# Expert layer: three of the eight in_b heads summed by TensorE through diagonal matrices, five left on VectorE

## The reference

```
sim = einsum('pbnhd,hkpd->pbnhk', q, keys)          # q = x @ Wq.T, 2 x 8 heads, 128 keys each
indices = best pair of keys of each head            # TOPK = 1: one expert of 8192 per head
A_in, B_in, A_out, B_out = in_a[indices], in_b[indices], out_a[indices], out_b[indices]
hidden = x @ W_in.T                                 # 1024 wide
lin = einsum('bnd,bnhkd->bnhk', x, A_in) * relu(scores)
hidden = hidden + einsum('bnhk,bnhkd->bnd', lin, B_in)
hidden = gelu(hidden)
out = hidden @ W_out.T
lout = einsum('bnd,bnhkd->bnhk', hidden, A_out) * relu(scores)
out = out + einsum('bnhk,bnhkd->bnd', lout, B_out)
```

## Time and profile before

| | |
|---|---|
| runs | 2763.74 us (2760.53 to 2766.83) |
| the profiled execution | 2771.96 us |
| its span in the trace | 2770.0 us |
| VectorE busy in the span | 2087.9 us (75%) |
| TensorE busy in the span | 2423.2 us (87%) |
| TensorE's granted clock, mean | 0.972 |
| rounds of experts | 32, from about 1590 us to the end |

### The profile page before, as it was taken

The page is one execution under the profiler, slowest core; times in us unless marked ns, Lnnn a source line. Parts: engine busy times, 40 slices in busy tenths (PEclk is TensorE's granted clock), DMA queues, the critical chain, the costliest instruction groups (busy, mean ns, idle before and its releaser), DMA issues. The chain is left out here.

```text
span 2770.0 us, 47172 instructions
## 1 busy us (share of the span) xinstructions
PE 2423.2 (87%) x12792; PEld 1326.1 (48%) x12792; DVE 2087.9 (75%) x5831; ACT 1093.2 (39%) x2559; POOL 1026.1 (37%) x1486
## 2 busy tenths in 40 slices
PE   7889988989889898899885999998989898989975
PEld 4455555655556555565543644443434343434432
DVE  1567676676766667667642299999989998999998
ACT  2266666666666566666663211111111111111110
POOL 1133333233332333323231245554545444545553
PEclk9999999999999999999987999999999999999997
DMA  3044454434544445444444899998989998999996
GB/s 103 17 119 116 118 161 132 138 111 118 161 132 137 112 118 159 132 138 114 147 137 143 302 372 377 370 372 337 373 331 375 351 372 331 375 366 346 375 369 255
DMA packets 303980, 631.15 MB, mean 228 GB/s; under 512 B 162800, under 2 KB 167920, under 8 KB 303728
## 3 DMA queue, kind: packets, MB, share of 16 engines
q0 software_dynamic: 79616, 423.66, 39.8%
q1 hardware_dynamic: 190320, 103.92, 13.3%
q10 hardware_dynamic: 33792, 100.67, 11.0%
HBM read 581.99 MB, written 146.80 MB: 263 GB/s over the span
## 5 line engine op out<-in xcount | busy, mean ns | idle before, releaser
L1078 DVE CUSTOM_DVE_ANT_0 scores<-s_bank,added 128x512 f32<-128x512 f32 x512 | 350.6, 688 | 273.2 <-PE s_bank L581 190.2
L1407 PE MATMUL l_bank<-fold,xn_tf 128*128 128x512 f32 x1024 | 449.9, 592 | 2.8 <-ACT xn_tf L1482 2.8
L886 ACT ACTIVATE probs<-scores,nmx 128x512 f32<-128x512 f32 x512 | 372.8, 728 | 151.8 <-DVE nmx L1078 147.9
L1367 POOL DMA_INDIRECT out_rows<-rows_out,rows_now x256 | 270.0, 1054 | 361.2 <-DVE out_sum L1631 286.6
L892 ACT COPY prob_t<-t_bank 128x512 f32<-128x512 f32 x512 | 298.4, 583 | 211.0 <-PE t_bank L591 211.0
L519 POOL TENSOR_TENSOR added<-mask_add,band 128x136 f32<-128x136 f32 (+1 forms) x512 | 245.9, 482 | 363.5 <-DVE nmx L1078 362.2
L1358 POOL DMA_INDIRECT in_rows<-rows_in,rows_now x256 | 296.1, 1157 | 224.9 <-PE hid_ps L1429 135.6
L591 PE MATMUL t_bank<-ident,probs 128*128 128x128 f32 x2048 | 316.4, 282 | 8.8 <-ACT cv L864 4.1
L591 PEld LDWEIGHTS t_bank<-ident,probs 128*128 128x128 f32 x2048 | 235.4, 142 | 180.9 <-issue 104.5
L1611 DVE CUSTOM_DVE_ANT_0 out_rows<-out_rows,hid,gates 128x1024 f32<-128x1024 f32 x256 | 320.0, 1279 | 2.7 <-ACT hid L1509 2.7
L1495 ACT COPY sims<-l_bank 128x512 f32<-128x512 f32 x128 | 74.2, 580 | 626.4 <-PE l_bank L1407 626.4
(11 more groups left out here) (177 smaller groups left out, 3607.4 us busy)
## 6 DMA issues: line engine op xcount, KB each, us to landing
rows_in<-in_in_b_dram ACTq DMA_DIRECT2D x16, 2048.0 KB, 9.2
rows_out<-in_out_a_dram ACTq DMA_DIRECT2D x16, 2048.0 KB, 9.2
rows_in<-in_in_a_dram ACTq DMA_DIRECT2D x16, 1024.0 KB, 5.7
rows_out<-in_out_b_dram ACTq DMA_DIRECT2D x16, 1024.0 KB, 5.5
x_scratch<-x SPq DMA_DIRECT2D x32, 512.0 KB, 7.4
rel_scratch<-rel_pad SPq DMA_DIRECT2D x16, 640.0 KB, 3.3
band<-rel_scratch SPq DMA_DIRECT2D x512, 20.0 KB, 2.1
prob_scratch<-probs SPq DMA_DIRECT2D x512, 20.0 KB, 2.4
```

Of the source, the lines that this page charges most:

```text
L886: nc.scalar.activation(prob_tile(s % PSLOTS), scores[:, s % 2, :], ACT.Exp, bias=nmx[:, s:s + 1], scale=-1.0, accum_out=lsum[:, s:s + 1]). ...
L1078: nc.vector.tensor_tensor_reduce(out=scores[:, s % 2, :], in0=s_bank[s % HPT][:, 0:L], in1=added[:, s % 2, :], scale=-1.0, scalar=-NEG, op ...
L1367: nc.gpsimd.indirect_dma_start(out_rows[:, h, :], None, rows_out, bass.IndirectOffsetOnAxis(rows_now[:, odd, h:h + 1], 0)).then_inc(out_lo ...
L1407: ins = nc.tensor.matmul(l_bank[c % 2][:], xn_t[:, k, :], fold[:, k, c * BANK:(c + 1) * BANK], start=(k == 0), stop=(k == KD - 1))
```

## The change

Of the eight in_b heads, VectorE sums heads 0 to 4 instead of 0 to 5, and TensorE takes heads 5 to 7 instead of 6 and 7.

```
-    VE_HEADS = range(6)
-    PE_HEADS = range(6, HEADS)
+    VE_HEADS = range(5)
+    PE_HEADS = range(5, HEADS)
```

## The result

The changed kernel takes 2779.16 us (median of 5 runs, 2777.41 to 2780.50) against 2763.74 us for the kernel before (5 runs, 2760.53 to 2767.65). The ratio is 1.0047, with a 95% interval of 1.0034 to 1.0060: slower, by 15.4 us of medians. The forecast was 2774.5, range 2762 to 2786, with 0.71 for slower.

The account below looks back on a forecast made before the run. VectorE was taken to bound the expert rounds, with TensorE and DMA close. Terms -0.7 (ordinary), +8.2 (after turns), +0.7 (first), +2.5 (last two) gave +10.7 us, 2774.5 on the median; range 2762 to 2786.

Parts of the forecast that it names:

- The race in an ordinary round: TensorE's `hid_filled` against VectorE's first sum: usable 2.68 us later, so VectorE waits 0.95 us.
- The cover: In an ordinary round before the change, `hid_filled` is usable 1.73 us before VectorE's first sum asks for it.
- The two terms ahead of them: Ahead of the added matmuls: waiting for a third product, 0.67 us, and ScalarE's third diagonal, 0.30 us; 0.97 together.
- The freed sum: One sum fewer on VectorE per round: gains 0.98 us, not 1.20, because it hid the wait behind `largest(2)`.
- The rounds after a turn: Five rounds following a turn of the loop, little or no cover left: +1.70 four times and +1.41, together +8.2 us.
- What was cost at nothing: TensorE's extra 1.71 us a round, `dense_out` with 4.90 us of cover, and gathers starting 2.7 us later: no time charged.
- the last two rounds: No search there and VectorE already waits for `hid_ps`: 2.68 less 1.43, +1.25 us each, +2.5 together.
- Rival D: Half clock covers the added records too: +8.5 us in five rounds, up to +3.4 in the last two, about 2786; 9%.
- the ordinary rounds: 24 rounds, each gaining 0.98 us and losing 0.95: a gain of 0.03 each, -0.7 us together.
- the wait behind `largest(2)`: On VectorE, the following `find` waits 0.15 us once the sum between them is removed.
- Rival A: `hid_filled` is usable before +7.87, so VectorE never waits for it inside the body: -31 us, about 2732; 5%.
- The pause at the turn (B): VectorE's five loop pauses, 26.4 us, change with code length; gone entirely 2748; 3%. The main forecast kept them.

Follow-up runs that it names:

- two more matmuls: Kernel before with the two diagonal matmuls of head 7 done twice, VectorE keeping six sums; ratio 1.0042, 2776.1 us.
- TensorE's part alone: Kernel before with three heads (6, 7, 5) through diagonals on TensorE while VectorE still sums six; ratio 1.0209, 2821.3 us.
- diagonals announced one by one: Changed kernel with each diagonal announced by itself, so TensorE starts head 5 as soon as its diagonal is written; ratio 0.9923, 2746.2 us.
- VectorE's part alone: Kernel before with five sums on VectorE and still two heads on TensorE, head 5 left out of the result; ratio 0.9902.
- the filler: Changed kernel with 12 unused 128x512 matmuls ahead of TensorE's wait for the diagonals, last two rounds only; ratio 1.0031, 2773.8 us.
- the moved code: Changed kernel with 100 unused semaphore increments at the start of VectorE's expert program; ratio 1.0026, 2771.1 us.

## Why the prediction was right

The race in an ordinary round was right in its terms, and each was measured apart. The cover: 1.71 us of matmuls alone cost an ordinary round nothing (two more matmuls). (The row of 3.53 us for eight records would make it 1.76; measured, it is 5.41 less 3.70, the 1.71 that was taken.) The two terms ahead of them, the third product and the third diagonal: with them the sum came 0.93 late (TensorE's part alone, and after), and with the diagonals announced one by one it came on time. The freed sum is worth 0.96 (VectorE's part alone; 0.98 forecast), and the net is -0.01 to -0.03 in ten rounds that have neither a turn at their end nor an added wait (2 to 5, 9, 13, 17, 21, 25, 27); round 28 is 0.19 shorter, since its first sum came 0.16 late before.

The rounds after a turn came out at +7.40 for +8.2, but this is right as a sum only, and in part luck. The forecast was +1.70 four times and +1.41; measured are 0.23 to 2.20 and 2.82. Against a run at full clock the slow part cost 2.28, 2.44, 2.95, 3.01 and 1.45 us before, and 1.63, 2.92, 2.28, 1.51 and 2.83 after: it differs by 1.5 us from round to round in either kernel, by the moment at which the clock comes back. The added records at full clock hold on average, not in each round. In the two other versions with the same order of work there (the filler, the moved code) the five rounds are +6.0 and +5.6.

What was cost at nothing cost nothing in ordinary rounds. TensorE no longer waits for the gelu except in the last round. `dense_out` was waited for once, 1.08 us in the last round, and that is not nothing: the kernel before has no such wait. The gathers, 2.7 us later, delayed no product: the waits ahead of L1590 are the pauses at the turn and a first one of 0.21.

Two terms were too small. They fall short by 2.7 and 2.95 us, the rounds after a turn give 0.8 back, and that is the 4.9 us between +10.7 and +15.6. First, the last two rounds: +5.23 for +2.5. The prediction took the added records there at full clock, and `dense_out` at nothing. The clock was at its lower level for longer: the slow part cost 1.41 and 1.93 us before, and 2.88 and 2.05 now (twelve records in 8.29 and 7.46 us instead of 5.41). That is 1.6 us. The other 1.08 is the wait for `dense_out` in the last round. Its row there, before and after:

```profile
2754.22 8.55 PE L1447 MATMUL out_ps<-w_out,hid_t 128*128 128x512 f32 x16 [0.68 <-ACT hid_t L1514]
```

```profile
2758.73 10.18 PE L1447 MATMUL out_ps<-w_out,hid_t 128*128 128x512 f32 x16 [0.68 <-ACT hid_t L1514]
```

An ordinary round has it in 7.13. With the filler that wait is gone as well, so both parts hang on the clock. Rival D had priced the records at up to 3.4 us; the filler removes 6 us, more than the change had added. Second, the ordinary rounds: +2.25 for -0.7. Seven of them (6, 10, 14, 18, 22, 26, 29) together have +2.32, because the wait behind `largest(2)`, forecast at 0.15, is 0.50 there; round 1 has +0.30, with 0.23 of waiting ahead of its last sum. The wait behind `largest(2)` was named as a second idle time, but its size was read from the chunk after, where it is always 0.15; with the code moved it is 0.15 in every round.

Rival A (the cover is enough) needed the two terms of 0.97 to vanish. That is what the split of the diagonals does, and there the gain of 0.94 to 0.96 a round appeared. The pause at the turn (B) stayed in every version, 4.0 to 6.4 us. The Trainium skill ("Runtime: NRT & Kernel Launch", "Instruction fetch mechanics") says that a taken branch to code outside the blocks held waits for a fetch. The traces agree that the pause stays, and no run here shows that it is a fetch.

## What to carry to other kernels

Work taken off the busiest engine is gained only if what that engine waits for does not come later by more than its cover: write down, from the start of a round, when the result is usable now and when it is asked for, and compare the delay with that difference, not with the other engine's idle share. When a batch of inputs is announced by one semaphore, a third member delays the first; announce them one by one before giving the engine more of them. And an instruction between a writer and its reader hides their wait: count what its removal uncovers. Where a change leaves an idle time, move such an exposed instruction into it. Two cures for one idle time do not add up.

## What the runs showed of the hardware beyond that

TensorE's clock fell to its lower level in the middle of the round loop after a wait of only 1.95 us for the diagonals, in six rounds of the version with six heads on VectorE and three on TensorE (10, 14, 19, 22, 26, 28), but in no ordinary round of the changed kernel, which waits 0.85 to 1.39 at the same place. It cost 1.70 us each time. It also fell in three rounds (7, 11, 27) of VectorE's part alone, behind a wait of 2.10: eight records took 5.39 us instead of 3.69 at a granted clock of 0.68, and this cost no time, because the cover of 1.73 was just enough. Other rounds with the same wait kept their clock; what tells them apart stays open. A wait of VectorE for its own result, of the same two instructions, was 0.50 us in seven rounds and 0.15 in the others, and 0.15 in all of them once 100 instructions stood ahead.
